# A score ring of five banks and a repeated maximum pair in the last unit of attention

## What is computed

```python
q = rope(heads(x @ Wq.T + bq)); k = rope(heads(x @ Wk.T + bk)); v = heads(x @ Wv.T + bv)
scores = softmax(einsum('bhqd,bhkd->bhqk', q, k) / sqrt(256), axis=-1)
x = layernorm(x + (einsum('bhqk,bhkd->bhqd', scores, v) -> tokens) @ Wo.T)
h = silu(x @ w1.T * s1) * (x @ w2.T * s2)
h = gelu(h @ h1.T * t1); h = gelu(h @ h2.T * t2)
out = layernorm(x + h @ w3.T * s3)
```

## Time and profile before

| | |
|---|---|
| median of 3 runs | 3811.35 us (3811.04 to 3815.56) |
| the profiled execution | 3821.48 us, of which the span is 3819.9 us |
| PE busy | 3526.6 us (92%) |
| DVE busy | 2932.8 us (77%) |
| ACT busy | 2462.1 us (64%) |
| PE's mean granted clock | 0.948 |

### The profile page before, as it was taken

How to read it: one execution, slowest core, us unless ns; L and a number is a source line. 1 busy time by engine, 2 the same in 40 slices (tenths; PEclk the granted TensorE clock), 3 DMA queues, 4 the chain that set the end, 5 groups by cost and what they waited for, 6 DMA issues and landing times. The chain is left out here.

```text
span 3819.9 us, 63480 instructions
## 1 busy us (share of the span) xinstructions
PE 3526.6 (92%) x20130; PEld 1516.0 (40%) x20130; DVE 2932.8 (77%) x3148; ACT 2462.1 (64%) x4472; POOL 196.4 (5%) x352
## 2 busy tenths in 40 slices
PE   8569999999999999999999999999998869999999
PEld 3223333333333333332333333333332158888887
DVE  6698999899899989998998999899983035555554
ACT  2118888788888878888887888788886512222222
POOL 3200000000000000000000000000000011111100
PEclk9759999999999999999999999999997589999999
DMA  8940000000000000000000000000000051111100
GB/s 208 212 137 12 12 12 12 13 12 12 23 12 12 12 13 12 12 12 17 18 12 13 12 12 12 12 12 23 8 8 4 3 182 35 34 34 44 40 17 12
DMA packets 64516, 125.61 MB, mean 33 GB/s; under 512 B 12551, under 2 KB 24904, under 8 KB 63032
## 3 DMA queue, kind: packets, MB, share of 16 engines
q1 hardware_dynamic: 59528, 114.02, 10.6%
q0 software_dynamic: 4704, 7.81, 0.7%
HBM read 90.59 MB, written 41.16 MB: 34 GB/s over the span
## 5 line engine op out<-in xcount | busy, mean ns | idle before, releaser
L646 DVE TENSOR_REDUCE group_max<-wide 128x2 f32<-128x1024 f32 x2048 | 2406.0, 1219 | 277.9 <-PE wide L507 277.6
L624 ACT ACTIVATE probs<-scores 128x512 f32<-128x512 f32 x4096 | 2223.3, 595 | 524.6 <-PE scores L572 431.5
L572 PE MATMUL scores<-q_sb,k_all 51*128 51x512 f32 x4096 | 1053.5, 511 | 148.6 <-ACT probs L624 62.7
L532 PE MATMUL sums<-probs,v_all 128*17 128x512 f32 x8192 | 1117.7, 619 | 0.0
L572 PEld LDWEIGHTS scores<-q_sb,k_all 51*128 51x128 f32 x4096 | 391.7, 188 | 1384.3 <-ACT probs L624 1355.7
L507 PE MATMUL wide<-k_all,q_sb 48*128 48x512 f32 x4096 | 807.3, 459 | 76.3 <-DVE group_max L646 50.2
L507 PEld LDWEIGHTS wide<-k_all,q_sb 48*128 48x128 f32 x4096 | 397.9, 191 | 394.8 <-DVE group_max L646 363.8
L1029 ACT ACTIVATE whole_hid<-acc,scale 128x512 f32<-128x512 f32 x128 | 84.6, 688 | 346.8 <-PE acc L910 346.7
L910 PE MATMUL acc<-hid_b,h2T 128*128 128x512 f32 x1024 | 241.6, 397 | 0.0
L910 PE MATMUL acc<-hid_a,h1T 128*128 128x512 f32 x1024 | 240.2, 395 | 0.0
L532 PEld LDWEIGHTS sums<-probs,v_all 128*17 128x17 f32 x8192 | 137.4, 96 | 258.2 <-ACT probs L624 150.7
(11 more groups left out here) (77 smaller groups left out, 1156.9 us busy)
## 6 DMA issues: line engine op xcount, KB each, us to landing
k_all<-k_parts SPq DMA_DIRECT2D x96, 128.0 KB, 5.0
q_sb<-q_parts SPq DMA_DIRECT2D x192, 64.0 KB, 2.3
w_words<-ff_weights SPq DMA_DIRECT2D x32, 352.0 KB, 3.1
q_parts<-parts SPq DMA_DIRECT2D x16, 512.0 KB, 5.6
k_parts<-parts SPq DMA_DIRECT2D x16, 512.0 KB, 6.2
heads<-mixed SPq DMA_DIRECT2D x32, 256.0 KB, 2.5
heads_sb<-heads SPq DMA_DIRECT2D x8, 1024.0 KB, 4.9
shares<-shares_dram POOLq DMA_DIRECT2D x112, 64.0 KB, 2.3
```

Of the source, the lines that this page charges most:

```text
L532: last = pe.matmul(sums[32 * j:32 * j + HD + 1, :], v_all[:, g, kt, j], probs[(kt * HG + j) % RING][:], start=(kt == 0), stop=(kt == KT - 1))
L572: pe.matmul(scores[(s + e) % BANKS][:], k_all[rows, g * GP + j, kt * P:(kt + 1) * P], q_sb[g][rows, j], start=True, stop=True).then_inc(sc ...
L624: act.activation(probs[n % RING][:], scores[s % BANKS][:], ACT.Exp, scale=INV_SCALE)\
L646: dve.reduce_max(group_max[:, n], wide[n % 2][:], AX_X).then_inc(wide_free, 1)
```

## The change

In the last unit the PE function `unit` is replaced by `last_unit`. Its score ring has five banks: the three of `scores` and both halves of `wide0`. A pair waits for the exponential of the score five places before its second score, that is the first exponential of the pair before the last; the first two pairs wait for the end of the unit before. Behind the first pair of every key tile it issues one pair of maximum matmuls into `wide1`, always with the first 128 queries and the first 512 keys; nobody reads the result, and it carries no semaphore. ACT reads the score of the last unit from the same ring of five. The other 31 units, and all stages before and behind, keep their instructions.

```diff
+        last_banks = [scores[b][:] for b in range(BANKS)] + [wide[0][:, e] for e in range(PAIR)]
...
+            def last_unit(g):
+
+                u = UNITS - 1
+                pe.wait_ge(shift_in, u * 96 + 192)
+                pe.wait_ge(wide_free, 2 + UNITS * MAXG)
+                for kt in range(KT):
+                    for j in range(GP):
+                        n = kt * HG + j * PAIR
+
+                        if n + PAIR > len(last_banks):
+                            pe.wait_ge(exps_done, u * SLOTS + BANKS + n + PAIR - len(last_banks))
+                        else:
+                            pe.wait_ge(exps_done, u * SLOTS + min(n + PAIR, BANKS))
+                        for e in range(PAIR):
+                            rows = slice(e * HALF, e * HALF + SLOT)
+                            pe.matmul(last_banks[(n + e) % len(last_banks)], k_all[rows, g * GP + j, kt * P:(kt + 1) * P],
+                                      q_sb[g][rows, j], start=True, stop=True).then_inc(scored, 1)
+                        if j == 0:
+
+                            for e in range(PAIR):
+                                rows = slice(e * HALF, e * HALF + SHIFT_ROW)
+                                pe.matmul(wide[1][:, e], q_sb[g][rows, j, 0:P], k_all[rows, g * GP + j, 0:CH],
+                                          start=True, stop=True)
+                    if kt > 0:
+                        sum_over(u, g, kt - 1, False)
+                    else:
+                        sum_over(u - 1, g - 1, KT - 1)
...
-            for g in range(1, NG):
+            for g in range(1, NG - 1):
                 unit(NCH - 1, g, left=min(2, NG - 1 - g))
+            last_unit(NG - 1)
             sum_over(UNITS - 1, NG - 1, KT - 1, False)
...
-                    act.activation(probs[n % RING][:], scores[s % BANKS][:], ACT.Exp, scale=INV_SCALE)\
+                    bank = last_banks[n % len(last_banks)] if last else scores[s % BANKS][:]
+                    act.activation(probs[n % RING][:], bank, ACT.Exp, scale=INV_SCALE)\
                         .then_inc(exps_done, 1)
```

## The result

| | median, us | lowest to highest | runs |
|---|---|---|---|
| before | 3811.68 | 3811.04 to 3815.56 | 4 |
| after | 3752.23 | 3749.43 to 3754.78 | 4 |

The ratio is 0.9842, with a 95% interval of 0.9825 to 0.9859: 1.6% faster, 59.5 us between the medians. The forecast was 3746.5, the range 3741 to 3758.

A forecast was written before the change was run, and what follows sets the result against it. It took the last unit to be bound by PE at half clock plus a 0.75 us wait for ACT per tile. One tile at 3.63, the rest at 2.03, gained 64.8 us: 3811.35 to 3746.5 us, range 3741 to 3758.

The forecast's parts named there:

- The ring of three made PE wait, and the ring of five ends that.: Last unit: second scores wait 0.75 us per key tile for ACT's exponential; with five banks that wait goes.
- PE's and ACT's tile: Last unit at full clock: PE needs 1.99 to 2.09 us a key tile, ACT 1.96 to 2.26.
- My 2.03 with 0.04 for hand-overs: Last unit: time taken per key tile at full clock, 0.04 above PE's sum; bounds 1.96 and 2.27.
- ACT's copy at the start of the unit: Start of last unit: ACT's 0.60 us copy holds up the first sums, exposed by 0 to 0.6, taken as 0.2.
- rival A: Last unit: ACT is the bound at 2.27 us a tile, 7.4 us less gain, 3754 us; chance 10%.
- The clock: Last unit: one tile at half clock, 3.63 us, then gapless PE work raises the clock to full and holds it.
- rival B: Last unit: the clock falls again and again, mean tile 2.83 us, 24.8 us less gain, 3771 us; chance 8%.
- The added pair: Last unit: 32 unread pairs, each 0.24 us of PE's time at full clock, 0.47 at half, without cover.
- The end: End of attention: last copy of the sums at 2988.8 instead of 3053.62, gain 64.8 us; what follows is chained to it.
- Moves as a whole: Behind attention: the feed-forward net starts from the same state and shifts earlier with its length unchanged.
- The reference: Whole kernel: the profiled 3821.5 lay 10 us above the median; the gain was taken from the median of 3811.35.
- The sum was 64.8 us: Whole gain: the last copy of the sums starts at 2988.8 instead of 3053.62.

The follow-up runs named there:

- the pair alone: The changed kernel with the unread pair kept but the ring of three instead of five: 3772.89 us, ratio to before 0.9899.
- the second trace of after: The changed kernel, unedited, run and traced again; the clock fell ahead of the last unit: 3756.94 us.
- ring only: The changed kernel with the ring of five but without the unread pair: 3750.96 us, ratio to before 0.984.
- the second trace of before: The kernel before, unedited, run and traced again: 3813.97 us, ratio to before 1.0004.

## Why the prediction was right, and where it was off

*The ring of three made PE wait, and the ring of five ends that.* Right: the earlier trace rows had 0.75 idle in every tile, after has none, and with the pair alone 0.51 is left, at full clock.

*PE's and ACT's tile.* PE 1.99 forecast, 1.88 measured in the tiles that catch up, where the second scores to the sums take 0.33 instead of 0.43; ACT 1.96 forecast, 1.96 measured, and it is the bound. My 2.03 with 0.04 for hand-overs was too long by 0.07, 2 us over the unit: from first scores to the last copy the sum gave 68.2 us, the second trace of after 66.3. ACT's copy at the start of the unit, for which I took 0.2, costs PE nothing that shows there: no row of PE has an idle time beside it. The pair of 1.09 for two exponentials did carry over to a long series, and rival A is out. The Trainium skill's figures (ScalarE: Activation LUTs, What ACT_TABLE_LOAD costs), from which an interval of 0.52 us could be estimated, were 0.03 above the 0.49 of the earlier trace rows and of this trace; by them the tile would be 2.08, so the measurement decides.

*The clock.* It held, as said. In the first trace of after it had not fallen, so there was nothing to come up from; I had one tile at half clock in every execution. That tile is there in the second trace, 3.42 for 3.63. But the reason that I gave for its holding, that PE is left no idle time, is not what it takes: the pair alone held it with 0.51 us of idle time in 2.65. And the swinging clock of rival B, with the rule behind it (the Trainium skill, TensorE: Matmul & The Clock Gate, A second HAM failure mode: psum-queue depth-cycling), was seen in none of the kernels with a longer ring or a pair: the clock of each stays at 1.00 from its rise, or from the start, to the end of the last unit, while its scores go round three, four or five banks.

*The added pair.* I costed it as PE's time and had the ring carry the gain. Both true, but I did not ask what the change would be without it. Without the ring it would be worth 39 us. Beside the ring it buys nothing while the clock is up (62.56 us with and without), and that it shortens the ramp where the clock has fallen is not shown. Its mere 128 instructions bring the two slow turns, 2.5 to 2.9 us behind attention. The medians of after and ring only cannot be told apart.

*The end.* "Moves as a whole" was the step that failed: the stretch behind the last copy is 2.4 to 2.9 us longer. The tile, 2 us too long in the sum, made up for most of this, which is luck.

*The reference.* The sum was 64.8 us. Counted from copy to copy the last unit gave 66.2, the unit before gave 1.3 against the second trace of before, and the net took back 2.9; that leaves 64.6, or 61.4 with the second trace of after, in which the clock fell. The medians gave 59.5. A second part went ahead of the change: the copy of the sums that begins the last unit but one stands at 2834.12 and 2835.85 in the two traces of after, at 2832.38 and 2831.55 in those of before, 1.7 to 4.3 us later with the same instructions. Over all traces of the study it lies between 2829.15 and 2835.85; what moves it was not looked into. The rest lies in what I took for constant too: my trace of before was one in which the clock fell early, and it was 10 us above its median, while both kernels' executions differ by whether and when it falls in the six tiles without maxima. One trace of each could not show that. I put the whole gain against the median, and named no term for it.

## What to carry to other kernels

Where an engine's clock depends on what it does, look for the stretch in which one kind of its work runs out: the wait that was hidden beside that work can then be paid twice, once as idle time (21 us here) and once by the clock on everything else (45 us here). Take away the wait first, with buffers that the ended work has left free, and start where the work ends, not at the next loop boundary; filler work gave 39 us here, but the ring alone gave 61. And count instructions that "cost nothing": 128 of them made a loop far off 2.5 to 2.9 us longer.

## What the runs showed that I had not expected

- In a gapless series ACT's exponentials take 822 ns each in the record, against 0.60 us in the units before, and still one starts every 0.49 us. The recorded length of an instruction is not its cost when the next one has started before its end. The row gives the shortest, median and longest in ns:

```profile
L656 ACT ACTIVATE probs<-scores x71: 672/822/845, 2920.8 to 2977.5; 128x512 f32<-128x512 f32 x71
```

- The clock fell about 2915, before 2906, or not at all, with the same instructions in the same order. Nor did it come up after a fixed stretch of work without idle time: 3.9 us in one trace, 9 to 10 in another.
- PE stalled 1.2 to 1.8 us at a loop's turn with 128, 160 or 288 instructions more ahead of the loop, and with 256 more it did not.
- 160 semaphore increments on PE took some 22 us, which is 0.14 us each.
